# Mixing the experts' projections on TensorE instead of VectorE, and waiting for constants where they are first read

## The reference

```python
pooled = hidden_states.mean(axis=1)
logits = relu(pooled @ Wg1 + bg1) @ Wg2 + bg2
vals, idx = top_k(logits, 2)
weights = zeros_like(logits).at[arange(B)[:, None], idx].set(softmax(vals))
def moe_proj(W, b):
    Wc = einsum('be,ecd->bcd', weights, W)      # four experts, 128x128 each
    bc = weights @ b
    return einsum('btc,bcd->btd', hidden_states, Wc) + bc[:, None, :]
q, k, v = moe_proj(Wq, bq), moe_proj(Wk, bk), moe_proj(Wv, bv)
```

## Time and profile before

| | |
|---|---|
| median of 3 runs | 543.93 us (543.71 to 546.2) |
| the profiled execution | 544.46 us, span 542.7 us |
| PE busy | 463.6 us, 85% |
| ACT busy | 364.0 us, 67% |
| DVE busy | 341.5 us, 63% |
| POOL busy | 159.4 us, 29% |
| mean granted TensorE clock | 0.948 |

### The profile page before, as it was taken

The page is one execution under the profiler, slowest core; times in us unless marked ns, Lnnn a source line. Parts: engine busy times, 40 slices in busy tenths (PEclk is TensorE's granted clock), DMA queues, the critical chain, the costliest instruction groups (busy, mean ns, idle before and its releaser), DMA issues.

```text
span 542.7 us, 16729 instructions
## 1 busy us (share of the span) xinstructions
PE 463.6 (85%) x6656; PEld 384.1 (71%) x6656; DVE 341.5 (63%) x1012; ACT 364.0 (67%) x898; POOL 159.4 (29%) x397
## 2 busy tenths in 40 slices
PE   3644766877789899899999999999999999999894
PEld 2433654654468678688888787878887879889793
DVE  2388778688636687786889897575675364323111
ACT  4435353958775868777778768887886776575352
POOL 6334022021143032645453114111430352233202
PEclk9999876799877999999999999999999999999798
DMA  7800000000000000000000000000000000000000
GB/s 244 352 18 5 1 17 8 11 5 8 13 2 2 7 7 8 2 18 7 2 6 13 7 7 7 18 8 7 7 14 6 7 4 16 2 11 2 11 2 10
DMA packets 11236, 12.19 MB, mean 22 GB/s; under 512 B 1984, under 2 KB 10520, under 8 KB 10776
## 3 DMA queue, kind: packets, MB, share of 16 engines
q1 hardware_dynamic: 11160, 11.13, 6.3%
HBM read 8.50 MB, written 1.05 MB: 18 GB/s over the span
## 4 chain that ended last, share of the span: by engine, by line
PE 61%; DVE 15%; ACT 11%; issue 4%; POOL 4%; DMA 2%; SPq 1%; POOLq 0%; DVEq 0%; ACTq 0%
PE bk L592 18%; PE bk L582 7%; DVE negmax L985 6%; ACT w1f L750 5%; PE bk L641 5%; PE bk L642 4%; PE bk L643 4%; PE bk L568 3%; PE bk L544 3%; PE bk L507 2%; ACT qk L736 2%; PE bk L485 2%; DMA hf<-in_half 2%; PE bk L560 1%; DVE wc L898 1%
## 5 line engine op out<-in xcount | busy, mean ns | idle before, releaser
L592 PE MATMUL bk<-w2f,hT 128*128 128x128 f32 x1024 | 137.3, 278 | 1.4 <-ACT hT L776 1.3
L776 ACT ACTIVATE hT<-bk,pk 128x256 f32<-128x256 f32 x256 | 107.1, 477 | 39.4 <-PE bk L643 39.1
L592 PEld LDWEIGHTS bk<-w2f,hT 128*128 128x128 f32 x1024 | 125.9, 194 | 4.7 <-ACT hT L776 2.0
L750 ACT ACTIVATE w1f<-bk 128x512 f32<-128x512 f32 (+1 forms) x192 | 98.5, 599 | 19.4 <-PE bk L568 18.8
L985 DVE TENSOR_REDUCE negmax<-bk 128x4 f32<-128x512 f32 (+1 forms) x192 | 104.8, 612 | 8.6 <-PE bk L568 8.1
L915 DVE SCALAR_TENSOR_TENSOR acc<-bk,comb,acc 128x128 f32<-128x128 f32 x128 | 38.8, 345 | 80.2 <-PE bk L592 79.7
L641 PE MATMUL bk<-yhi,w1hi 128*128 128x256 f16 x256 | 71.2, 278 | 0.0
L642 PE MATMUL bk<-ylo,w1hi 128*128 128x256 f16 x256 | 70.9, 277 | 0.0
L643 PE MATMUL bk<-yhi,w1lo 128*128 128x256 f16 x256 | 70.8, 277 | 0.0
L1025 POOL TENSOR_SCALAR shift<-mv 128x2 f32<-128x2 f32 x40 | 9.3, 233 | 198.5 <-DVE mv L925 197.4
L582 PE MATMUL bk<-w1f,val 128*32 128x128 f32 (+1 forms) x1536 | 57.2, 295 | 8.1 <-ACT w1f L750 7.7
(11 more groups left out here) (149 smaller groups left out, 758.4 us busy)
## 6 DMA issues: line engine op xcount, KB each, us to landing
w1f<-in_w SPq DMA_DIRECT2D x1, 2048.0 KB, 14.0
w2f<-in_w SPq DMA_DIRECT2D x1, 2048.0 KB
pk<-in_pack SPq DMA_DIRECT2D x1, 1788.5 KB, 7.7
qk<-mT SPq DMA_DIRECT2D x96, 16.0 KB, 1.8
xin<-in_x SPq DMA_DIRECT2D x8, 128.0 KB, 2.6
out<-outb SPq DMA_DIRECT2D x8, 128.0 KB, 1.8
cin<-in_ctx SPq DMA_DIRECT2D x8, 77.0 KB
hf<-in_half SPq DMA_DIRECT2D x1, 384.0 KB, 9.7
```

Of the source, the lines that this page charges most:

```text
L592: last = mm(o[:, i * D:(i + 1) * D], hT[:, k % HRING, i * T:(i + 1) * T], w2f[:, k, :], start=c == 0 and i == 0, stop=c == CH - 1, skip_gr ...
L750: act.activation(probs[0:nk, ring(n, q), :], bank(g, st, q)[0:nk, :], ACT.Exp, scale=SCALE[L]).then_inc(s_exp, 1)
L776: act.activation(hT[:, k % HRING, :], bank(g, st)[:, m * W:(m + 1) * W], ACT.Relu, bias=P("b1")[:, k:k + 1]).then_inc(s_relu, 1)
```

## The change

The mix of B's weights leaves DVE. The four experts' weights are packed so that strip r of PSUM rows 32r to 32r+31 of the result is one matmul: contraction over 128 rows that hold 32 input rows of each of four experts, a 128 x 32 left side `mixT` (the identity pattern `fold` scaled by each expert's weight), and 387 columns, the three projections and three bias columns. Eight such matmuls (two sequences, four strips) make a new step `B.mix` between `top` and `B.qk`; they go to two banks, and ACT copies both into `wc`. The biases are columns of `wc`. DVE in `top` now computes weight, normaliser and `mixT`. In the diff stand DVE's part, then PE's and ACT's part of `B.mix`.

```diff
+def mixers(g, s):
+    chosen = pick(g, s, E0)
+    dve.tensor_reduce(psumw[s][:], chosen, X_AXIS, ALU.add)
+    link(dve.tensor_tensor(pm[s][:], chosen, P("own").unsqueeze(1).to_broadcast((128, SPS, E0)), ALU.mult))
+    dve.reciprocal(lmax[s][:], psumw[s][:])
+    link(dve.tensor_reduce(gsel[s][:], pm[s][:], X_AXIS, ALU.add))
+    for i in range(SPS):
+        last = dve.tensor_scalar(mixT[s][:, i, :], P("fold"), gsel[s][:, i:i + 1], lmax[s][:, i:i + 1],
+                                 ALU.mult, ALU.mult)
+    last.then_inc(s_mixT[s], 1)
...
-                        link(weigh(g, s, E0, gw[s][:]))
-                        mix(g, s)
+                        mixers(g, s)
...
+                if h == "B.mix":
+                    banks = [o] + [take_bank(pe, g, st, i) for i in range(1, SPS)]
+                    pe.wait_ge(s_mixT[s], g + 1)
+                    for i in range(SPS):
+                        for r in range(4):
+                            last = mm(banks[i][32 * r:32 * r + 32, 0:MIXW], mixT[s][:, i, :],
+                                      P("w0")[:, r * MIXW:(r + 1) * MIXW], start=True, stop=True)
+                        if i < SPS - 1:
+                            last.then_inc(s_mixed[s], 1)
...
+                if h == "B.mix":
+                    for i in range(SPS):
+                        if i < SPS - 1:
+                            act.wait_ge(s_mixed[s], (SPS - 1) * g + i + 1)
+                        else:
+                            act.wait_ge(s_hop[s], hop(g, h))
+                        last = act.activation(wc[s][:, i, :], bank(g, st, i)[:, 0:MIXW], ACT.Copy)
+                    last.then_inc(s_read[s], 1)
```

```diff
             load(0, 0)
-            sp.dma_start(pk[:, a:b], pack[:, a:b]).then_inc(s_first, 16)
-            for s in range(1, LANES):
+            sp.dma_start(pk[:, 0:b], pack[:, 0:b]).then_inc(s_first, 16)
+            load(0, 1)
+            sp.dma_start(pk[:, b:c], pack[:, b:c]).then_inc(s_gate, 16)
+            for s in range(2, LANES):
                 load(0, s)
-            sp.dma_start(pk[:, b:], pack[:, b:]).then_inc(s_const, 16)
+            sp.dma_start(pk[:, c:], pack[:, c:]).then_inc(s_const, 16)
...
-                if not const and kind == "ln1" and st[2] == "B":
+                if (g, st) == FIRST_GATE:
+                    act.wait_ge(s_gate, 16)
+                elif (g, st) == FIRST_MIX:
                     act.wait_ge(s_const, N_CONST * 16)
...
-                elif kind == "y":
+                elif kind == "hop" and st[2] == "D.cT":
                     pool.wait_ge(s_y[s], g + 1)
...
-                elif kind == "hop" and st[2] == "D.yT":
-                    pool.wait_ge(s_read[s], read(g, "D.yT"))
+                elif kind == "top" and st[2] == "D":
                     pool.tensor_tensor(ylo[s][:], yT[s], yhi[s][:], ALU.subtract).then_inc(s_y16[s], 1)
...
 ORDER = (
-    "0202010231020001110120102102112105100555020300522550053203013103021020302320302231020301301202020103"
+    "0020020310121001120310100210252231503005503002052152501205130233200113021003102210202032001203102000"
```

More of the change, by code:

```diff
@@ L136, in uses @@
         return 1 + step[2] % 2
+    if step[2:] == ("B.mix",):
+        return SPS
     return int(kind in ("hop", "moe_start") or kind == "PV" and step[3] == 0)
@@ L171 @@
 N_MOE = 2
+FIRST_GATE = next(x for x in STEPS if x[1][2:] == ("B.hid",))
+FIRST_MIX = next(x for x in STEPS if x[1][2:] == ("B.mix",))
 def build(nc, x, ctx, pack, rows, half, w1, w2, b2, out):
@@ L930, in _ @@
             dve.wait_ge(s_init_dve, LANES)
-            const = False
             for g, st in STEPS:
                 kind, s = st[0], st[1]
-                if not const and kind == "ln1" and st[2] == "B":
+                if (g, st) == FIRST_GATE:
+                    dve.wait_ge(s_gate, 16)
+                elif (g, st) == FIRST_MIX:
                     dve.wait_ge(s_const, N_CONST * 16)
-                    const = True
                 if kind == "ln1":
@@ L1046, in rows_of @@
                 return R(name).unsqueeze(1).to_broadcast((128, n, D))
-            const = False
             for g, st in STEPS:
                 kind, s = st[0], st[1]
-                if not const and kind == "ln1" and st[2] == "B":
+                if (g, st) == FIRST_GATE:
+                    pool.wait_ge(s_gate, 16)
+                elif (g, st) == FIRST_MIX:
                     pool.wait_ge(s_const, N_CONST * 16)
-                    const = True
                 if kind == "ln1":
@@ L1056, in _ @@
                     scales(mv[s], ve[s], rstd[s], shift[s]).then_inc(s_rstd[s], 1)
-                elif kind == "hop" and st[2] == "B.hid":
+                elif kind == "hop" and st[2] == "A.pT" and g == 0:
+                    pool.memset(val[s][:], 0.0).then_inc(s_val[s], 1)
+                    pool.wait_ge(s_val[s], 1)
+                    pool.memset(val[s][:].rearrange("p n (r c) -> p n r c", r=2)[:, :, :, 2 * HD:3 * HD], 1.0
+                                ).then_inc(s_val[s], 1)
+                elif kind == "hop" and st[2] == "B.v":
                     pool.wait_ge(s_xn[s], norm(g, "B"))
@@ L1157 @@
             "dq": heads(a["L1_ffn_Wq"])[:, put], "dk": heads(a["L1_ffn_Wk"])[:, put], "dv": heads(a["L1_ffn_Wv"]),
-            "wg2": a["L0_ffn_Wg2"], "gate": a["L1_ffn_gate_W"], "bg1": a["L0_ffn_bg1"].reshape(-1, 1), "b0": b0,
+            "wg2": a["L0_ffn_Wg2"], "gate": a["L1_ffn_gate_W"], "bg1": a["L0_ffn_bg1"].reshape(-1, 1),
+            "bg2": np.tile(a["L0_ffn_bg2"], (128, 1)), "own": own, "fold": fold,
             "b1": a["L1_ffn_b1"].reshape(UNITS, 128).T, "cos": cos, "sin": sin,
```

146 lines of the change are left out of this document (60 added, 86 removed).

## The result

The changed kernel takes 539.17 us in the median of 10 runs (536.0 to 542.92), the kernel before beside it 543.86: a ratio of 0.9917 with a 95% interval of 0.9887 to 0.9946, 4.5 us or 0.8% faster. The forecast was 536.2 us, in a range of 527 to 548. The profiled execution of the changed kernel took 541.94 us, with a span of 540.1, which is 2.8 us above its median; the profile of before lies 0.6 above its own. A difference of the two profiles is therefore smaller than that of the medians.

What follows compares the result with a forecast made beforehand. DVE was taken to set the pace mid-fill, PE to bound from 164 us. From the profiled 544.46: - 4.0 - 6.5 + 6.1 - 2.3 - 1.0 = 536.8, less 0.5 for the median: 536.2; range 527 to 548.

Steps and rivals of the forecast that it cites:

- The start: Up to lane 0's first `B.qk`: earlier gate and waits bring it to about 30 from 33.9; 4.0 us less, bounds 0 to 6.
- The price of the mix: On PE, strips run side by side as in `PV`: 1.53 us a job at full speed, 3.0 at the lower.
- Switching between strips and the full array: On PE around each mix: going in and out costs some 0.05 us, left out of the sum.
- rival 4: Each tiling switch on PE empties the array: up to 0.44 us a job, 1.8 us in the second round, 538; chance 0.15.
- rival 3: The strips do not overlap with 387 columns: 5.3 us a job on PE, above 565; chance 0.05.
- The mix in the second round: In PE's saturated stage from 164 us, four mixes of 1.53 us count in full: 6.1 us more.
- each microsecond added to PE counts in full: After 164 us, where PE is the bound, added PE work lengthens the kernel by its whole time.
- Relief of the second round: Between 164 and 330 us, less DVE work removes a quarter of PE's 9.0 us idle: 2.3 us less, bounds 0 to 6.
- Relief of the first round: In the fill, 34 to 164 us, three mixes leave DVE; half of 12.9 us counts: 6.5 us less.
- POOL at block D: Ranks go ahead of three element-wise operations, so D's gate ends sooner: 1.0 us less, bounds 0 to 3.
- Rival 1: DVE sets the whole fill's pace: 12.9 us come in full, start 6, second round 4, giving 526; chance 0.18.
- Rival 2: ACT and the lanes' chains set the fill's pace: DVE's relief brings nothing, ACT's copies add 4 us, 550; chance 0.17.

Runs made afterwards that it cites:

- start-only kernel: The kernel before with only the changed kernel's loads, waits and `val` fills; mix on DVE, old order and banks: 540.95 us against 545.4, ratio 0.9926.
- warm start: The changed kernel with identity matmuls on PE in its waits of the first 36 steps: 534.03 us against 544.8, ratio 0.9805.
- doubled mix: The changed kernel with the mix's eight matmuls issued twice in the second round, same values again: 544.07 us, ratio 0.9949.
- hybrid: The changed kernel, same order and banks, with first-round mixes on PE and second-round mixes on DVE, weights loaded in a second layout: 554.16 us, ratio 1.0173.
- the further step from 0.89 to 0.91: The changed kernel with identity matmuls on PE in the first 36 steps and at six more places of the fill: 534.09 us, ratio 0.9799.
- the fillers: Identity matmuls on PE in the first 36 steps; added to the kernel before with only its start changed, mix on DVE: 542.95 us, ratio 0.9948.
- lane 0 first: The changed kernel with lane 2's context transpose ordered behind lane 0's first transpose: 538.11 us, ratio 0.9879; with all fillers 534.29 us, ratio 0.9742.

## Why the prediction was right, and where its sum was not

The range held the time, and the answer (faster by over 0.5%) came true. The gain was put at 7.7 us and was 4.5. The answer rests on the start: it gives 4.0 us by itself, and the balance of relief and new work, on which most of the forecast was spent, came out near nothing. Point by point:

- **The start, 4.0 us: right.** 4.0 by the start-only kernel (2.6 to 5.4), though that one has its mix on DVE, and the marks in its profile lie only 1.2 to 1.7 us before those of before. `B.qk` was forecast at about 30 and stands at 30.54; the terms show singly: the rank at 25.00 (forecast 25.3), the mix at the lower clock 2.81 (3.0), ACT's copy 0.49 (0.49). The moved `val` fills brought nothing, as costed: lane 0's normalisation begins at 7.05, before at 7.21.
- **The price of the mix: right.** Forecast 1.53 us from the `PV` rows, measured 1.44 or 1.32 (next point). The four strips run side by side with 387 columns too; rival 3 (5.3 us) is out.
- **Switching between strips and the full array (rival 4): a small price is there.** The time from a mix's start to the start of the next instruction is 1.44 us where that one uses the full array, and 1.32 where it is `PV` in the same strips:

```profile
221.90 0.66 PE L526 MATMUL bk<-pk,po 128*128 128x128 f32 x4
222.48 1.51 PE L464 MATMUL bk<-pk,mixT 128*32 128x387 f32 x16
223.92 0.28 PE L659 MATMUL bk<-yhi,w1hi 128*128 128x256 f16 x1
...
283.75 1.51 PE L464 MATMUL bk<-pk,mixT 128*32 128x387 f32 x16
285.07 1.06 PE L601 MATMUL bk<-w1f,val 128*32 128x128 f32 x32
```

  The mixes at 254.35 and 302.21 repeat this (1.44 before the full array, 1.32 before `PV`), and so do the four in the profile of the kernel with the warm start (1.44, 1.44, 1.33, 1.32). So leaving the strips costs 0.12 us. Entering costs some 0.08: the four records of L526 before the mix hold the engine 0.58 us, and 0.50 where a full-array step follows at 262.64 (both 0.66 us long, their ends modelled). That is 0.2 us in and out, under the 0.44 of rival 4. The forecast's own 0.05 was misread: its two rows give 2 x 1.01 - 1.93 = 0.09. By the rule of the Trainium skill (TensorEngine Tiling (Array Packing), Key Properties) a change of tiling mode drains the engine; the trace agrees in that a change costs something, but whether it is a drain or the loading of a wider left side, no run here separates.
- **The mix in the second round, + 6.1 us: somewhat high.** Two times 1.44 and two times 1.32 are 5.5 us of work. The doubled mix says that 4.4 of 5.2 us of such work arrive, so some 4.7. The step "each microsecond added to PE counts in full" nearly holds.
- **Relief of the second round, - 2.3 us: not to be separated.** PE's idle time fell by 2.6 us there. But the hybrid shows that "a quarter of the idle time" was the wrong way to price it: in the new order, taking DVE's mix out of the second round is worth about 14 us net of PE's share, in the old order DVE's mix left PE idle 9.0 us only. What a block on DVE costs is set by what the written order has put behind it, not by DVE's busy share.
- **Relief of the first round, - 6.5 us: it came, and was not kept.** Lane 3 ends its first round 10.7 us earlier than in the start-only kernel and its second 1.3 us later. All terms but the start were to sum to - 3.7 us; measured are - 0.5, give or take 2. The term that was mis-sized is the price of the first-round mixes on PE. The sum let three of them hide in the 38 us that PE had to spare in the fill. But the four take 9.9 us there, three of them at the lower level, and PE's busy time from 34 to 164 us rose by 8.9 us against before. At 505 us the start-only kernel and the changed one have done the same steps, within 1.3 us. Up to there PE waits 9.7 us less in the changed kernel (66.8 to 57.1) and works 9.7 us more (438.2 to 447.9), and the eight mixes alone are 16.0 us of work:

```profile
164.00:505.00 341.00, 326.52 (x4873) 277.52 (x4872) 225.06 (x674) 254.26 (x628) 108.34 (x264) 0.99 0.03 8
```

```profile
164.00:505.00 341.00, 328.73 (x4891) 276.93 (x4890) 203.00 (x623) 256.44 (x633) 103.53 (x254) 0.99 0.03 8
```

  (The start-only kernel first, then the changed one.) So what the relief gave back, the mixes took up, in the fill as in the second round; this is read from the sums, and no run varies the first-round mixes by themselves. A lower clock than before is not the reason, since counted with the unrecorded part the fill has 65 us at the lower level after, 65 before and 68 in the start-only kernel. That PE pays double for the mixes at that level is shown by their lengths, and that a higher clock would have helped fits the warm start: 29 us at the lower level, and 6.1 us less time. But its start changed with it, and the further step from 0.89 to 0.91 gained nothing, so how much of the 6.1 is the fill's clock stays open.
- **POOL at block D, - 1.0 us:** the waits fell from 10.4 to 3.3 us, as foreseen; its share of the time was not tried by itself.
- **Rival 1** (all relief in full, 526) did not come true even for the first round, whose end came 12.4 us earlier; the forecast's start and first round make 10.5 and the rival's 18.9. **Rival 2** (slower through ACT, 550) did not happen. ACT's copies moved into the chain, its line on `w1f` being 30.6% of the stretch from 84 to 97 us where DVE's maxima had been 61.6%. But the largest part of that chain is now PE's own: its four lines sum to 56.3%, where they were 14.5%, the mix and `B.qk` at half speed (1.99 and 2.00 us) among them. The forecast weighed DVE against ACT, and the engine that took over the pace there was PE. PE's longest waits in the fill are still for DVE:

```profile
by line: ACT w1f L778 30.6%; PE bk L504 15.4%; PE bk L464 15.3%; PE bk L601 13.4%; PE bk L587 12.2%; issue 6.0%; ACT po L785 3.7%; ACT qk L764 3.7%
```

```profile
PE bk L522 <- DVE m L1008: 6.4, 3, 3.5
PE bk L601 <- ACT w1f L778: 2.9, 5, 1.1
```

- **The marker was badly chosen.** The first `moe_start` was to come near 153 and came at 165.29 (165.54 before), which the prediction would have read as rival 2. The new order only puts more of the other lanes' work in front of it; PE is busy 8.9 us more in that stretch. A marker has to be a point with the same work before it in both kernels.

What stays open: whether a faster PE in the fill would also help the kernel with its mix on DVE, since the fillers did not change its clock there; how much of the warm start's gain is the fill's clock; and what the new order alone is worth, since every way of taking the mix out of it or putting it into the old one also changed the list of banks, except the hybrid. The figure that can be given is joint: mix on PE with its order against mix on DVE with the old, both with fillers in the start, 0.9805 against 0.9948, or 7.8 us (give or take 3), and that holds for fillers that reach the fill in one kernel only. Against the start-only kernel without fillers, 0.9926, it is 6.6 us (give or take 2.8).

## What to carry to other kernels

Where the order of steps and the banks are written out by hand, moving work off an engine is worth what the new order makes of it: price a block by what is queued behind it, and change one string at a time. Idle time of the engine that bounds the kernel later need not be free room: price what you hide in it, at the speed that the engine has there. Read that speed from the lengths of like instructions as well as from the granted clock, which here read full for up to 60 us of half speed. A few matmuls into banks that are overwritten anyway cost little. And judge a gain in the middle of a kernel by the work that remains, not by one lane's clock.

## What the runs showed that was not expected

- **Matmuls added to the waits of the start made the kernel 6 us faster** (0.9917 to 0.9805). With them the granted clock 34 to 164 us in was 0.89 in the profile and not 0.75, and the first mix ran at full speed; that this is how they gain is likely and not isolated. In the start PE was busy 24.0 us of 34, against 18.4. The Trainium skill (TensorE: Matmul & The Clock Gate, HAM oscillation — how this bites in real kernels) describes an engine whose clock falls in waits for transfers; here the clock fell with the DMA engines busy 3% of the stretch, and PE's longest waits in it were for DVE and ACT. In the kernel with its mix on DVE, where PE still waits 3.16 us ahead of `B.qk`, the same fillers had no effect (0.9926 to 0.9948); that this wait is the reason was not tested.
- **The end has a dip of its own.** After the last lane's mark PE waits 1.6 us, runs for some 2 us and waits again. In the profile of before its clock falls during that run, for some seven microseconds; in that of the changed kernel it does not, with the same instructions: the same eight records take 2.04 and 1.13 us. First before, its timeline and the stretch from 510 us, then the changed kernel:

```profile
508.46 2.04 PE L592 MATMUL bk<-w2f,hT 128*128 128x128 f32 x8 [0.71 <-ACT hT L776]
```

```profile
510.00:520.00 10.00, 10.00 (x76) 9.16 (x75) 1.29 (x5) 4.19 (x10) 0.00 (x0) 0.81 0.05 13
```

```profile
508.51 1.13 PE L611 MATMUL bk<-w2f,hT 128*128 128x128 f32 x8 [1.03 <-ACT hT L804]
```

  That is the whole of the 2.6 us between the two spans; up to 505 us the two profiled executions stand level. It belongs to the execution and not to the kernel: over all fourteen profiles the time from the last mark to the end is 37.7 to 37.9 us in six (the changed kernel with lane 0 first among them), 35.8 to 36.0 in three and 35.2 to 35.3 in five.
- **The list of PSUM banks alone is worth 43 us** (0.9926 to 1.072), with the same instructions in the same order: ten times the change under study. Which of its waits make up the 43 us was not traced.
- **The granted clock in the views starts late.** It reads 1.00 until its first record at full speed, 60 us into the profile of before, while the matmuls take twice their time (2.00 against 0.91 us). So mean clocks of kernels with different starts, 0.948 and 0.929 for before and after, are no measure of who ran slower.
